# Moving the first token stores behind the first gathers, and two pairs of buffers swapped, in a fused cross-attention and mixture-of-experts kernel

## The reference

```python
x = x + jnp.tanh(g_xattn[0]) * _L0_xattn_ref(ctx_1024, _layernorm(x, axis=-1))
x = x + jnp.tanh(g_ffn[0]) * _L0_ffn_ref(_layernorm(x, axis=-1), L0_ffn_gate_w, L0_ffn_expert_w)
```

## Time and profile before

| what | value |
|---|---|
| median of 3 runs | 600.76 us |
| the profiled execution, and its span | 601.94 us, 600.2 us |
| PE busy | 455.1 us (76%) |
| DVE busy | 307.4 us (51%) |
| ACT busy | 263.0 us (44%) |
| POOL busy | 221.4 us (37%) |
| PE in the 40 slices of 15 us | `8989655477132303674998999999999999999980` |
| granted PE clock in the same slices | `9999976667665656697997999999999999999995` |
| DMA in the same slices | `8965334530047001359999687878868787778742` |

### The profile page before, as it was taken

The page is one execution under the profiler, slowest core; times in us unless marked ns, Lnnn a source line. Parts: engine busy times, 40 slices in busy tenths (PEclk is TensorE's granted clock), DMA queues, the critical chain, the costliest instruction groups (busy, mean ns, idle before and its releaser), DMA issues. The chain is left out here.

```text
span 600.2 us, 8209 instructions
## 1 busy us (share of the span) xinstructions
PE 455.1 (76%) x2022; PEld 271.3 (45%) x2033; DVE 307.4 (51%) x1635; ACT 263.0 (44%) x508; POOL 221.4 (37%) x214
## 2 busy tenths in 40 slices
PE   8989655477132303674998999999999999999980
PEld 8989543254032201331543644444444444444440
DVE  7778799999988885898289511011111010111000
ACT  5538787854836402981473232223333322233320
POOL 5550221000000000002434475766657666766532
PEclk9999976667665656697997999999999999999995
DMA  8965334530047001359999687878868787778742
GB/s 293 350 189 185 85 84 123 181 98 2 0 157 264 1 1 46 142 206 364 369 229 296 104 167 138 143 127 145 134 122 149 132 143 138 133 125 150 117 56 35
DMA packets 61434, 88.88 MB, mean 148 GB/s; under 512 B 24981, under 2 KB 25237, under 8 KB 61229
## 3 DMA queue, kind: packets, MB, share of 16 engines
q0 software_dynamic: 16048, 37.31, 35.4%
q1 hardware_dynamic: 40813, 42.65, 22.2%
q10 hardware_dynamic: 4528, 8.41, 4.2%
HBM read 48.92 MB, written 39.43 MB: 147 GB/s over the span
## 5 line engine op out<-in xcount | busy, mean ns | idle before, releaser
L1967 PE MATMUL psum<-big,tokens 128*128 x560 | 256.2, 601 | 2.9 <-ACT tokens L1626 2.9
L703 POOL DMA_INDIRECT stage<-x_rows,row_ids x71 | 70.0, 985 | 236.6 <-issue 186.1
L1967 PEld LDWEIGHTS psum<-big,tokens 128*128 128x128 f32 x560 | 102.5, 193 | 105.9 <-issue 105.9
L1322 DVE TENSOR_TENSOR part_scale<-stage,st 128x1 f32<-128x1 f32 x62 | 10.0, 162 | 199.4 <-DMA stage<-x_rows,row_ids 199.4
L723 POOL DMA_INDIRECT out_dram<-prow,row_ids x34 | 57.3, 1686 | 39.9 <-ACT prow L1634 18.9
L723 POOL DMA_INDIRECT out_dram<-work,row_ids x36 | 57.2, 1589 | 32.0 <-ACT work L1634 11.5
L1634 ACT ACTIVATE work<-psum,tile_shares 128x512 f32<-128x512 f32 x36 | 24.7, 687 | 97.1 <-issue 73.2
L1634 ACT ACTIVATE prow<-psum,tile_shares 128x512 f32<-128x512 f32 x34 | 23.4, 687 | 92.8 <-issue 81.3
L1941 PEld LDWEIGHTS psum<-ident,stage 128*128 128x128 f32 x284 | 35.6, 143 | 45.7 <-issue 33.8
L1749 PE MATMUL psum<-ident,stage 128*128 128x128 f32 x128 | 29.4, 418 | 33.7 <-ACT big L1525 20.3
L1941 PE MATMUL psum<-ident,stage 128*128 128x128 f32 x284 | 43.8, 278 | 9.3 <-DMA stage<-x_rows,row_ids 8.8
(11 more groups left out here) (389 smaller groups left out, 650.9 us busy)
## 6 DMA issues: line engine op xcount, KB each, us to landing
tokens<-in_x_dram SPq DMA_DIRECT2D x16, 1024.0 KB, 13.2
stage<-in_L_ffn_expert_w_dram ACTq DMA_DIRECT2D x8, 1024.0 KB, 5.4
out_dram<-tokens SPq DMA_DIRECT2D x8, 1024.0 KB, 10.2
x_rows<-tokens SPq DMA_DIRECT2D x6, 1024.0 KB, 6.5
tokens<-dist_rows SPq DMA_DIRECT2D x52, 64.0 KB, 2.2
dist_rows<-work SPq DMA_DIRECT2D x16, 160.0 KB, 2.0
x_rows<-tokens SPq DMA_DIRECT2D x8, 256.0 KB, 6.7
dist_rows<-prow SPq DMA_DIRECT2D x5, 256.0 KB, 10.4
```

What stands on the lines that cost most here:

```text
L703: pool.indirect_dma_start(out=xin[:, n % UX, :], out_offset=None, in_=x1_d[0:T, :] if n < FA else x1_d[:, :], in_offset=bass.IndirectOffse ...
L1967: ins = nc.tensor.matmul(psum[:, UP + n % UP, :], xinT[:, n % UX, c, :], expT[:, bass.ds(own, 1), c, :].rearrange("p o d -> p (o d)"), sta ...
```

## The change

Six edits, in four engines' instruction streams:

- `xinT` moves from tiles 0 to 3 of `tokens` to `work`, and the four `yout` buffers in `work` move to tiles 0 to 3 of `tokens`.
- The x loads of groups 6 and 7 are issued together with those of 4 and 5 at L517.
- SP waits for gather(3) to have landed before the output stores of groups 0 to 3.
- DVE runs `first_shares` ahead of add_context(20) and (21).
- ACT no longer waits for the stores of group 0 ahead of copy_in(0).
- ACT waits for these two stores in copy_out(0).

```diff
-        xinT = x[:, 0:UX, :].rearrange("p h (c n) -> p h c n", c=CH)
+        xinT = work[:, :, :].rearrange("p h (c n) -> p h c n", c=CH)
...
             if k < 4:
-                return work[:, k, :]
+                return x[:, k, :]
...
-            for g in (GB, GB + 1):
+            for g in range(GB, NG):
                 sp.dma_start(x[:, GT * g:GT * g + GT, :], x_v[g]).then_inc(s_x[g], 16)
...
+            sp.wait_ge(s_xi[UX - 1], 16)
             for g in range(GB):
                 sp.dma_start(out_v[g], x[:, GT * g:GT * g + GT, :]).then_inc(s_out[g], 16)
-            for g in (GB + 2, GB + 3):
-                sp.dma_start(x[:, GT * g:GT * g + GT, :], x_v[g]).then_inc(s_x[g], 16)
...
             leave_first()
+            first_shares()
             for t in (20, 21):
                 add_context(t)
-            first_shares()
             place_choices()
...
                 act.wait_ge(s_y, n + 1)
+                if n == 0:
+                    act.wait_ge(s_out[0], 16)
+                    act.wait_ge(s_rows[0], 16)
...
-            act.wait_ge(s_out[0], 16)
-            act.wait_ge(s_rows[0], 16)
             copy_in(0)
```

## The result

The change makes the kernel slower: 606.95 us (median of 5 runs, 604.88 to 607.14) against 600.47 for the kernel before (5 runs, 599.11 to 601.95) on the same chip. The forecast was 596.3, its range ended at 600.2.

The account below looks back on a forecast made before the run. PE was taken as the bound, busy from 340 us on, so the end follows turn(9). Gain 4.5 - 0 - 0 - 0 = 4.5 us: profiled 597.4, median 600.76 - 4.5 = 596.3 us, own range 595.0 to 597.7, wider 593.2 to 600.2.

Parts of the forecast that it names:

- The gain is 4.5 us: First gathers without the stores: expert(0) begins at 281.3, not 285.78, and count follows; bounds 3.3 and 5.8 us.
- The wait on store 0: copy_out(0) on ACT: store 0 lands at 288.1, delaying it about 1 us; cost 0, with 2.2 us of cover.
- a sign of being right: On ACT, copy_out(0) is released by the store, not by the shares; forecast at 288.3.
- The x loads and the order of first_shares: Two more x loads issued at L517, and first_shares ahead of two adds on DVE: cost 0 each.
- turn(9) is due at 342.91 - 4.5 = 338.4. Covered by 1.7 us.: On PE: gather(9), issued near 332.9, lands near 336.7, ahead of turn(9).
- rival (d): SP and POOL chain from store 3 to gather(9): slower, 604.6 us if store 3 lands 10 us later; chance 0.10.
- What the stores do later: SP and POOL after 283.1: late stores delay add(0), gather(8) and pairs_out, but gather(9) stays covered; cost 0.
- SP's queue is now empty before 309: Argument against the slower SP and POOL chain: the queue was full from 305.86 in the kernel before.
- (a): Store 0 takes 10 us and holds copy_out(0), delaying expert(2): gain 1.7 us, time 599.1; chance 0.12.
- (b): First gathers are slow by themselves, not through the stores: saves 0.7 us, time 600.1; chance 0.08.
- (c): PE resumes at 277.8, about where its clock fell: gain 7.4 us in all, time 593.4; chance 0.10.
- Even turns by the prediction's estimate: DMA engines alternate between SP's store and POOL's gather: a gather's 0.66 us doubles, so the change saves 0.7 us.

Follow-up runs that it names:

- e2: The changed kernel without SP's wait on gather(3) ahead of the stores of groups 0 to 3: 601.96 us, ratio 1.0011.
- e7: The kernel before with the output stores of groups 6 and 7 behind pairs_out(1): 601.49 us, ratio 1.0001.
- e8: The changed kernel with 32 filler matmuls of 128x512 on PE ahead of turn(9): 602.63 us, ratio 1.0012.
- e15: e13 with 21 filler matmuls ahead of turn(0) and 4 ahead of turn(1): 598.41 us, ratio 0.9960.
- e6: The changed kernel with output stores of groups 6 and 7 behind pairs_out(1) and gathers 5 to 8 ahead of add(0): 597.08 us, ratio 0.9931.
- e12: e6 itself again, unchanged, on another chip: 600.51 us, ratio 0.9987.
- e13: e6 with SP waiting for gather(9) to land before the output stores of groups 6 and 7: 598.05 us, ratio 0.9967.
- e5: The changed kernel with the output stores of groups 6 and 7 behind pairs_out(1): 601.78 us, ratio 1.0017.
- e4: The changed kernel with gathers 5 to 8 ahead of add(0) on POOL: 602.71 us, ratio 1.0022.
- e1: The changed kernel with pairs_out(0) moved behind rows and outputs of groups 6 and 7, right ahead of pairs_out(1): 604.55 us, ratio 1.0055.
- e3: The kernel before with pairs_out(0) moved right ahead of pairs_out(1): 601.98 us, ratio 1.0015.

## Why the prediction was wrong

**Right.** "The gain is 4.5 us": count came 4.54 us earlier, and place_choices at 291.31 against "near 291.4". That it fits so closely is luck: expert(0) began at 280.63 and not at 281.3, and took 5.36 us where 4.74 were carried over, and these two misses cancel. Gathers 0 and 1 landed within the 3.3 to 4.8 us named (turn(0) starts 3.57 us behind gather(0)'s issue). The wait on store 0 cost nothing, though not as told: copy_out(0) was forecast at 288.3, released by the store, which was also named as a sign of being right. It began at 287.19, released by the shares, since the store went out at 282.49 and not at 283.1 and landed in 4.5 us and not 5. The x loads and the order of first_shares cost nothing that shows (e2, 1.0011 [0.9991, 1.0031]). The row numbers came 5.94 us earlier: the 4.5, and 1.4 us of expert(5), which took 6.71 us in the profiled execution before and 5.34 in this one, by the clock. The 1.4 are no gain of the change: in e7, which has the kernel before up to there, expert(5) took 5.39 us as well.

**The step that failed first: "turn(9) is due at 342.91 - 4.5 = 338.4. Covered by 1.7 us."** 342.91 is turn(10). On PE turn(n+1) goes ahead of expert(n), so turn(8) stands ahead of expert(7), and turn(9) is one expert sooner than taken. In the timeline of PE in the kernel before it is the third of these rows, and the row shown in the earlier trace rows is the next turn:

```profile
334.92 0.63 PE L1941 MATMUL psum<-ident,stage 128*128 128x128 f32 x4 [0.45 <-issue]
335.38 3.60 PE L1967 MATMUL psum<-big,tokens 128*128 x8
338.99 0.66 PE L1941 MATMUL psum<-ident,stage 128*128 128x128 f32 x4
339.48 3.60 PE L1967 MATMUL psum<-big,tokens 128*128 x8
```

Gather(9), issued at 335.60 with 3.3 us to landing, arrives at 338.9, and turn(9) starts at 338.99. It had no cover at all in the kernel before. With the right row the forecast's own times say so: landing 336.7 against a turn due at 338.99 - 4.5 = 334.5, 2.2 us late, which would have cut the gain to 2.3 us (599.6 for the profiled execution, 598.5 for the median) even with every size as forecast. The kernel before had little room for it: pairs_out(1) landed there at 323.96 + 9.5 = 333.5, less than 2 us ahead of the row numbers, so row numbers that come 4.5 us earlier leave pairs_out(1) as the last. The forecast's 332.9 for gather(9) took that in; its cover did not. The cover was the one thing that stood between the forecast and rival (d).

**Then the sizes of the chain, each of which was a term of "What the stores do later".** The forecast has gather(9) issued at 332.9; it was 337.56, 4.7 us later:

| step | forecast | measured |
|---|---|---|
| store 3 landed | 296.5 | 297.4 |
| gather(8) issued | 304.5 | 305.95 |
| pairs_out(0) issued | 308.6 | 313.39 |
| pairs_out(1) issued | 322.5 | 324.38 |
| pairs_out(1), us to landing | 9.5 | 12.3 |

The largest is the landing of gather(8): 4 us were taken, and pairs_out(0) followed its issue by 7.4. Of the 4.8 us by which pairs_out(0) was late, 1.9 were left at pairs_out(1), mainly since the issue of rows 6 took 2.89 us and not 5.98. The landing of pairs_out(1) added the other 2.8. The DMA engines were full: windows of the changed kernel have a DMA share of 0.97 from 300 to 310 and of 1.02 from 310 to 320. The argument of the prediction's own first step, that megabytes in the queue double a gather's time (8.2 us for 3.3), was not applied to this gather. "Against it: SP's queue is now empty before 309" was wrong in the same way: SP issued nothing from 302.3 on, but the engines were still at work on what it and POOL had issued.

**And the clock.** The prediction weighed it at the idle time that the change shortens, not at the one it may open. It put the later one at nothing, because it saw no idle time there. 2.3 us came from it (e8).

**The sum.** Turn(9) due at 334.5, began at 340.95: 6.45 us, of which 2.2 are the wrong row, 4.7 the later issue, and -0.4 a landing of 3.4 us instead of 3.8. The clock adds 2.3: 8.7 us. Forecast 597.4 for the profiled execution, measured 606.02: 8.6. By the medians the miss is 10.7 us, since the profiled execution before lies 1.2 us above its median and that of the changed kernel 0.9 us below. Three slips in the working are small and change nothing: the lower bound of the gain is 3.4 by its own sum and not 3.3, gather(1) landed 1.0 and not 0.8 us ahead of expert(0) (276.90 + 7.9 = 284.8 against 285.78), and four stores at the sizes named end at 296.2 and not at 296.5.

**The rivals.** (a) and (b) did not happen. (c), a kept clock, was seen in e15 and brought nothing there. (d) is what happened, though not by its own condition: it asked for store 3 to land 1.7 us late, and it was 0.9 late. It was too narrow, since it took one term of the chain for all, and its chance of 0.10 rested on the false cover.

**What stays open.** e6 and e12 are one kernel, and its runs lie between 595.87 and 604.59 us; e13's between 596.4 and 602.5, so that keeping the output stores away from gather(9) does not take the spread away. Why a store takes 7.9 us in one execution and 11.6 in another was not found. Nor was it found how the stores slow a gather. That its completion counts only when all stores issued before it are done does not fit: gather(0) of the kernel before landed 3.3 us ahead of the fourth store, and gather(9) of e5 was in by 336.79, where turn(9) starts, while the second output store, issued ahead of it at 326.4, took 11.9 us and landed at 338.3. Even turns by the prediction's estimate do not fit either. Something between them, such as a completion behind what an engine had already begun, or an uneven sharing of the bandwidth, was not measured apart.

## What to carry to other kernels

Before a wait is called covered, name by its number the instruction that covers it and count the instances on the timeline from the first; with a software-pipelined order, in which turn(n+1) goes ahead of expert(n), the next row of the same line is one iteration off. Here that was 3.9 us, and the cover was nothing. When large transfers are moved later in an in-order queue, look for the small transfer that stands behind them and is waited for: put it ahead of all bytes that nobody needs yet, and let those go when the awaited one has landed. An idle time that a change opens on PE costs its length and can cost the matmuls at half clock behind it: 2.3 us more behind the 7.72 us here, nothing behind the 2.12 us of e13.

## What the runs showed of the hardware

- A gather of 128 rows of 2056 bytes is at its reader 3.3 to 3.6 us after its issue with little beside it, and about 6.3 us beside two stores of 1 MB issued 4 to 10 us ahead of it (e5, e12). It takes 7.6 us beside two that went out 2.5 us ahead (gather(11) of e13), and about 8 behind four with more transfers of 1 MB beside them (before, e2). It can land ahead of a store issued before it: by 3.3 us in the kernel before. SP waited 7.4 us from the issue of gather(8) in the changed kernel, with rows and output of group 5, three gathers and adds in flight.
- Issuing can take the time and not only the transfer: rows of a group (1 MB) took 0.37 us to issue after 11 us in which SP had issued nothing (changed kernel, 301.35), and 9.28 us behind a `pairs_out` of 16 KB in pieces of 8 bytes and the megabytes ahead of it (e4); two `pairs_out` took 11.43 us (e1).
- After 7.7 us without a matmul PE was at 1.2 GHz (granted clock 0.50) up to 345, and expert(8) took 5.46 us for 3.60. And the same expert(5) took 6.71 us in the profile of the kernel before, 5.34 in that of the changed one and 3.70 in e3, after the same idle time of 2.85 us: one profiled execution and the next can differ by 3 us of clock that no edit explains.
